# Second transposing split of a two-layer Flamingo block: context rows normalised by two engines, and earlier release of the latents' buffers

## What is computed

```python
x = x + tanh(g_xattn[0]) * L0_xattn_ref(_layernorm(x), ctx, ctx, W_q, W_k, W_v, W_o, b_o)
x = x + tanh(g_ffn[0])   * L0_ffn_ref(_layernorm(x), w1, conv_w, conv_b, w2)
x = x + tanh(g_xattn[1]) * L1_xattn_ref(ctx, _layernorm(x), mask, g_x, b_x, g_l, b_l, Wq, Wkv, Wout, g_o, b_o)
x = x + tanh(g_ffn[1])   * L1_ffn_ref(_layernorm(x), Wg, W1, W2, W3)   # top 2 of 8 experts

# inside L1_xattn_ref:
xn = layer_norm(ctx, g_x, b_x)           # context rows: mean, variance, gain, bias
ln = layer_norm(latents, g_l, b_l)       # latents: x after two layers
kv = concatenate([xn, ln], axis=1) @ Wkv
```

## Time and profile before

| | us |
|---|---|
| the three runs | 1301.79, 1304.35, 1304.62 |
| median | 1304.35 |
| the profiled execution, device time | 1301.08 |
| span of its trace | 1299.4 |
| second split in it, end of feed-forward to first matmul of the long stage | 424.9 to 463.2 |

### The profile page before, as it was taken

The page is one execution under the profiler, slowest core; times in us unless marked ns, Lnnn a source line. Parts: engine busy times, 40 slices in busy tenths (PEclk is TensorE's granted clock), DMA queues, the critical chain, the costliest instruction groups (busy, mean ns, idle before and its releaser), DMA issues.

```text
span 1299.4 us, 36455 instructions
## 1 busy us (share of the span) xinstructions
PE 1039.3 (80%) x13489; PEld 821.8 (63%) x13489; DVE 889.0 (68%) x2508; ACT 877.5 (68%) x1832; POOL 868.5 (67%) x983
## 2 busy tenths in 40 slices
PE   0569899994987379999999999999999982478760
PEld 0445677772544258888887878778787862356640
DVE  5689788885787767677676667667776763455545
ACT  0559899992665468888887878778888871355540
POOL 1170699993666747778678788788888886255561
PEclk9959655555999589999999999999999995698985
DMA  9995000000122001112212222121222211222216
GB/s 220 258 284 125 7 16 16 16 16 6 34 43 52 5 2 34 35 27 31 47 35 51 39 39 56 29 61 34 49 42 39 52 35 57 74 71 69 70 38 194
DMA packets 181539, 78.15 MB, mean 60 GB/s; under 512 B 116137, under 2 KB 177620, under 8 KB 181371
## 3 DMA queue, kind: packets, MB, share of 16 engines
q1 hardware_dynamic: 161563, 61.71, 21.9%
q0 software_dynamic: 4544, 8.67, 2.2%
q10 hardware_dynamic: 15264, 5.51, 1.7%
HBM read 19.54 MB, written 30.47 MB: 38 GB/s over the span
## 4 chain that ended last, share of the span: by engine, by line
PE 45%; POOL 5%; DVE 4%; issue 4%; another core or an unknown queue 3%; ACT 2%; DMA 1%; SPq 0%; POOLq 0%; ACTq 0%; DVEq 0%
PE bank L1428 12%; PE bank L1476 6%; PE bank L1462 4%; PE bank L1458 4%; PE bank L1459 4%; PE bank L1460 4%; PE bank L1502 3%; PE bank L2083 3%; PE bank L1447 3%; PE bank L2096 2%; POOL tokens L1321 1%; DVE X L2180 1%; POOL attention_pl_l L1221 1%; POOL attention_pl_c L1221 1%
## 5 line engine op out<-in xcount | busy, mean ns | idle before, releaser
L1748 DVE TENSOR_REDUCE attention_negmax<-bank 128x2 f16<-128x410 f32 x256 | 137.6, 579 | 141.6 <-PE bank L1447 141.6
L1221 POOL TENSOR_TENSOR attention_pl_l<-attention_probs_l,attention_ph_l 128x512 f16<-128x512 f32 x128 | 148.4, 1159 | 90.6 <-ACT attention_ph_l L1605 88.4
L637 POOL TENSOR_TENSOR attention_probs_l<-attention_probs,attention_probs_h 77x512 f16<-77x512 f32 x128 | 145.3, 1152 | 53.0 <-ACT attention_probs_h L719 48.8
L1221 POOL TENSOR_TENSOR attention_pl_c<-attention_probs_c,attention_ph_c 77x512 f16<-77x512 f32 x128 | 147.8, 1155 | 0.0
L2202 POOL DMA_INDIRECT outputs<-layer_kv x78 | 82.4, 1056 | 76.4 <-ACT layer_kv L2138 56.5
L1462 PEld LDWEIGHTS bank<-identh,attention_negmax 128*128 128x128 f16 (+1 forms) x1024 | 84.0, 108 | 56.6 <-issue 1.6
L1428 PE MATMUL bank<-layer_kv,ah 128*128 128x128 f16 x1024 | 108.2, 220 | 4.4 <-PEq L2315 4.2
L1476 PE MATMUL bank<-attention_vh_l,attention_ph_l 128*128 128x65 f16 x512 | 95.8, 195 | 18.0 <-POOL attention_pl_c L1221 18.0
L1428 PE MATMUL bank<-v1h,layer_kv 128*128 128x256 f16 (+1 forms) x512 | 106.3, 275 | 1.8 <-DVE attention_vl_c L1755 1.8
L1742 DVE SCALAR_TENSOR_TENSOR attention_tl<-bank,attention_th 128x512 f16<-128x512 f32 x128 | 87.7, 685 | 22.1 <-ACT attention_th L1596 21.9
L1605 ACT ACTIVATE attention_probs_l<-bank 128x512 f32<-128x512 f32 x128 | 76.2, 596 | 37.9 <-PE bank L1462 37.1
(11 more groups left out here) (378 smaller groups left out, 4132.6 us busy)
## 6 DMA issues: line engine op xcount, KB each, us to landing
tokens<-blank SPq DMA_DIRECT2D x1, 18360.0 KB, 70.9
layer_kv<-tokens SPq DMA_DIRECT2D x39, 136.0 KB
ctx<-outputs SPq DMA_DIRECT2D x8, 512.0 KB, 5.5
X<-in_x SPq DMA_DIRECT2D x4, 512.0 KB, 9.3
attention_pay<-attention_pay SPq DMA_DIRECT2D x8, 256.0 KB
out<-X ACTq DMA_DIRECT2D x8, 256.0 KB, 4.8
attention_turned_h<-attention_heads_h SPq DMA_TRANSPOSE x96, 2.2
attention_turned_l<-attention_heads_l SPq DMA_TRANSPOSE x96, 2.4
```

Of the source, the lines that this page charges most:

```text
L637: pool.tensor_tensor(probs_l[:, n % SLOTS], probs[:, n % 2], probs_h[:, n % SLOTS], ALU.subtract).then_inc(p_split, 1)
L1221: last = pool.tensor_tensor(low[:, g % 2], whole[:, g % 2], high[:, g % 2], ALU.subtract)
L1748: last = dve.tensor_reduce(negmax[:, g, 2 * i:2 * i + 2], score[i], AX.X, ALU.max, negate=True)
```

## The change

- The context's normalising goes from GpSimd alone to GpSimd and ScalarE: for each chunk GpSimd does batches 0 and 1 of the four (`first_half`, `tensor_scalar` as before) and ScalarE batches 2 and 3 (`second_half`, `activation` with Identity and the same scale and shift). TensorE waits for both (`ready` and a new semaphore `other`).
- ctx gets depth 4 in place of 2, with banks 0, 1, 6 and 7. The x job keeps banks 2 to 5.
- ScalarE does the second halves of chunks 0 and 1 ahead of its loop, and that of chunk k + 2 ahead of the copies of chunk k. GpSimd does the first halves of chunks 0 to 2 ahead of its loop, and that of chunk k + 3 ahead of the low part of chunk k.
- TensorE raises `turned` of all jobs at the start of its program, not when it comes to each job.

```diff
-            job.banks = [bank[2 * at + u][:, 0:CH * rows].rearrange("p (c r) -> p c r", r=rows) for u in range(job.depth)]
+            of = [0, 1, 6, 7] if job.by == "both" else [2 * at + u for u in range(job.depth)]
+            job.banks = [bank[i][:, 0:CH * rows].rearrange("p (c r) -> p c r", r=rows) for i in of]
...
         def _(pe):
             for job in jobs:
+                pe.sem_inc(job.turned, job.depth)
+            for job in jobs:
                 def turn(k, u):
-                    if job.by:
+                    if job.by == "both":
+                        pe.wait_ge(job.ready, k + 1)
+                        pe.wait_ge(job.other, k + 1)
+                    elif job.by:
                         pe.wait_ge(job.ready, k + 1)
...
-                pe.sem_inc(job.turned, job.depth)
                 chunks(pe, job, turn)
...
         def _(act):
+            def second_half(job, k):
+                u = k % job.depth
+                act.wait_ge(job.turned, k + 1)
+                for c in range(CH // 2, CH):
+                    one = slice(k * CH + c, k * CH + c + 1)
+                    last = act.activation(job.normed[:, u, c], job.src[:, k * CH + c], ACT.Identity, bias=job.shift[:, one],
+                                          scale=job.rstd[:, one])
+                last.then_inc(job.other, 1)
...
                     chunk = bass.ds(k * CH, CH)
+                    if job.by == "both" and k + 2 < NCH:
+                        second_half(job, k + 2)
                     act.wait_ge(job.turned, k + job.depth + 1)
...
+                if job.by == "both":
+                    second_half(job, 0)
+                    second_half(job, 1)
                 chunks(act, job, copy)
...
         def _(pool):
+            def first_half(job, k):
+                u = k % job.depth
+                pool.wait_ge(job.turned, k + 1)
+                for c in range(CH // 2):
+                    one = slice(k * CH + c, k * CH + c + 1)
+                    last = pool.tensor_scalar(job.normed[:, u, c:c + 1], job.src[:, one, :], job.rstd[:, one], job.shift[:, one],
+                                              ALU.mult, ALU.add)
+                last.then_inc(job.ready, 1)
...
                     chunk = bass.ds(k * CH, CH)
+                    if job.by == "both" and k + 3 < NCH:
+                        first_half(job, k + 3)
                     pool.wait_ge(job.high, k + job.depth + 1)
                     pool.tensor_tensor(job.lo(chunk), job.whole[:, u], job.hi(chunk), ALU.subtract).then_inc(job.split, 1)
-                    if job.by == "gpsimd" and k + 2 < NCH:
-                        normalise(pool, job, k + 2, u)
 
                 pool.sem_inc(job.split, job.depth)
-                if job.by == "gpsimd":
-                    normalise(pool, job, 0, 0)
-                    normalise(pool, job, 1, 1)
+                if job.by == "both":
+                    for k in range(3):
+                        first_half(job, k)
                 chunks(pool, job, low)
...
-                              "gpsimd", rstd=w.rstd_c, shift=w.shift_c, gain=gain_x, bias=bias_x),
+                              "both", rstd=w.rstd_c, shift=w.shift_c, gain=gain_x, bias=bias_x, depth=4),
```

More of the change, by code:

```diff
@@ L415, in split_transposed @@
             job.whole = m.sb(f"whole_{n}", [128, job.depth, CH, rows])
+            if job.by == "both":
+                job.other = m.sem(f"other_{n}")
             job.ready, job.turned, job.high, job.split = (m.sem(f"{x}_{n}") for x in ("ready", "turned", "high", "split"))
-            job.banks = [bank[2 * at + u][:, 0:CH * rows].rearrange("p (c r) -> p c r", r=rows) for u in range(job.depth)]
+            of = [0, 1, 6, 7] if job.by == "both" else [2 * at + u for u in range(job.depth)]
+            job.banks = [bank[i][:, 0:CH * rows].rearrange("p (c r) -> p c r", r=rows) for i in of]
         chain = m.sem("chain")
@@ L436, in normalise @@
                 one = slice(k * CH + c, k * CH + c + 1) if isinstance(k, int) else bass.ds(k * CH + c, 1)
-                if job.by == "gpsimd":
[L438 to L441, removed]
+                last = eng.tensor_scalar(job.normed[:, u, c:c + 1], job.src[:, one, :], job.mean[:, one, 0:1], job.rstd[:, one],
+                                         ALU.subtract, ALU.mult)
             last.then_inc(job.ready, 1)
```

## The result

The changed kernel took 1292.71 us (median of six runs, 1290.36 to 1294.54) against 1303.07 us for the kernel before (six runs, 1298.3 to 1304.62). The ratio is 0.9924, with an interval of 0.9908 to 0.994: faster by some 10 us, where 3.5 us were forecast and the range ended at 1296.5. The direction was right, the size wrong by a factor of three. (The kernel before was measured at 1304.35 us when the forecast was made and at 1303.07 us beside the changed kernel, so 1.3 us of the distance between 1300.9 and 1292.71 are the base.)

The account below looks back on a forecast made before the run. GpSimd on ctx, then VectorE on x, then the tail bound the second split. VectorE ending 3.2 us earlier and a tail 0.3 us shorter gave 3.5 us: 1304.35 - 3.5 = 1300.9 us, range 1296.5 to 1304.2.

Parts of the forecast that it names:

- What bounds the kernel: Between the feed-forward and the long stage, the path is GpSimd on ctx (2.48 us per chunk), VectorE on x, then the tail.
- tail: Second split, from VectorE's end on x to GpSimd's last low part: 3.9 us in place of 4.2, 0.3 us less.
- Release at once: Second split: VectorE begins x right behind its last small step, at 438.52 in place of 444.18, minus 5.66 us.
- ScalarE's share: Second split: ScalarE's added activations at 0.41 us each, two per ctx chunk, make its period 1.84 us, which sets ctx's pace.
- GpSimd's tensor_scalar do no such thing: Second split: GpSimd's tensor_scalar don't stall VectorE; L53 began inside four of them and took 0.22 us.
- The size of collisions: Each VectorE stall beside a GpSimd tensor_tensor costs 0.75 us on normalisings, by the first split, and 0.87 on small steps.
- small steps end: Second split: VectorE's small steps meet the low parts of ctx chunks 3 and 4, two collisions, and end at 438.5.
- 32 normalisings without collisions: Second split: VectorE's work on x with no stall, 32 x 0.29 = 9.28 us.
- collisions on x: Second split: VectorE's normalising of x meets three ctx and six x low parts, 9 at 0.75, 6.75 us.
- rival A: Collisions cost nothing extra: VectorE's stalls are bounded by the buffers or hide in its waits; gain 5.7 us, 1298.7, chance 0.15.
- The rest of the program shifts whole: The long stage is the same work with the same data, its first 3 us at the lower clock as now.
- rival D: Slower: a shifted start adds long-stage stalls with clock falls, 4.2 us each; one more 1305.1, two 1309.3; chance 0.07.

## Why the prediction was wrong

From the 1300.9 us that I gave to the measured 1292.71 it is 8.2 us: 1.3 are the base, 2.4 the second split, where the sum had too high a price for VectorE beside GpSimd, and some 4.5 the long stage, which the sum had as unchanged.

**What bounds the kernel: right.** The path through the second split was GpSimd on ctx, VectorE on x and the tail, and speeding up ctx shortened it.

**Release at once: right in sum, wrong in cause.** The 5.66 us of idle time went. I booked them on the release; without it they go as well, and alone it saves 2.05 us. The text itself had what was needed to see that: it had TensorE free for x before 438.5, which is when VectorE's small steps were to end. What the 5.87 us are made of is this: 5.66 of idle time gone, 0.9 of shorter small steps, less 0.66 for one more collision on x.

**ScalarE's share: right.** 0.43 us per instruction (0.41 taken), ctx chunks 1.76 us apart (1.84), last ctx low part from 439.63 (440.2), no wait on the new semaphore that cost anything.

**"GpSimd's tensor_scalar do no such thing": the step that failed in kind.** I read it off one instruction, L53, that ran free, as did the five behind it. But the two slow steps of the same rows speak against it: L1103 and L57 began at 433.81 and 436.29, the `tensor_tensor` only at 434.11 and 436.59. At 0.2 us each they would have been done before it began, had the last `tensor_scalar` ahead of it not held them. With four buffers on GpSimd alone a hold went on through four `tensor_scalar`. When they hold VectorE and when they don't stays open.

**The size of collisions: the step that failed in the sum.** Its terms against the trace:

| term | predicted | measured |
|---|---|---|
| small steps end | 438.5 | 437.6 (held by 0.44 twice, not 0.87) |
| 32 normalisings without collisions | 32 x 0.29 = 9.28 | 8.2 (0.257 each) |
| collisions on x | 9 x 0.75 = 6.75 | 3 x 0.49 + 5 x 0.91 = 6.0 |
| VectorE on x in all | 16.0 | 14.24 |
| tail | 3.9 | 4.2 |

The measured collisions are the long instructions of the trace less the 0.333 of a free one (0.82 or 0.83 beside ctx, 1.23 to 1.26 beside x); the pace is what is left, (14.24 - 6.0) / 32. The pace of 0.29 and the price of 0.75 came from the first split: the pace is too slow and the price of a collision beside x too low, and the two errors cancelled for the 13.58 us of the kernel before, which the sum therefore seemed to explain. It counted six collisions there; the trace has seven, and eight in the changed kernel, not nine. The three differences are 0.9 + 1.8 - 0.3 = 2.4 us, and 3.5 + 2.4 is the 5.9 of the trace. The nearest of my cases for the split was rival A, 5.7 us, and not by luck alone: what x lost by one more collision (0.66 us) was less than what the small steps gained (0.9).

**The rest of the program shifts whole: wrong by more than that.** Two executions differ by up to three falls of the clock in attention, 597 to 600 us for the same kernel. I had the rows for it in rival D, but used them only for a slower kernel, and put the stall itself into the price; the stalls are there in every trace, and the fall alone costs 1.0 to 2.1 us. The range should have carried that scatter on the fast side: the lower end would have been 1298.7 - 4 = 1294.7 and still short of the 1292.7 that came. (By the terms it names, the range began at 1298.7 - 2.6 = 1296.1 rather than 1296.5, which changes nothing here.) Even with the right split, 1303.07 - 5.9 = 1297.2 would have been 4.5 us too high, and of these only a part is traced to falls.

## What to carry to other kernels

Before you book a wait on the semaphore that ended it, ask when the engine behind it would have been ready anyway: here the release looked like the cure, and with half of GpSimd's normalising on ScalarE it wasn't needed. When VectorE has a chain of short dependent instructions, take GpSimd's work away from beside it rather than queue more: prefetching deeper on GpSimd made this stage slower than before. A price and a pace fitted to one mix of work can be wrong in both; check them against the durations of single instructions. Before a gain of some microseconds is read out of two traces, look whether the clock fell equally often in both.

## What the runs showed of the hardware

- VectorE held by GpSimd: an instruction of 0.19 us took 3.06 us beside a `tensor_tensor`, four `tensor_scalar` and another `tensor_tensor` of GpSimd. In the kernel before, six small steps in a row ran free (0.18 to 0.22 us each) beside four `tensor_scalar`.
- The Trainium skill, SBUF — State Buffer, section "Who interferes with whom", describes the shared ports as an exclusive lock that one of the two engines has for a whole instruction. The rows agree for single holds: with four buffers on GpSimd alone, three small steps took 0.67 us each beside `tensor_tensor`s of 0.75. They also have a hold that lasted over several instructions and small steps that weren't held at all.
- One more collision of a 128x128 normalising costs VectorE 0.49 us beside the `tensor_tensor` of ctx and 0.91 us beside that of x.
- GpSimd is slowed as well: four `tensor_scalar` in 1.98 us beside VectorE's normalising, 1.78 beside the small steps.
- After a stall of TensorE of 2.1 to 2.5 us its clock fell to 1.2 GHz for 3.4 us in some executions and in others not, for the same kernel and the same stall. With one such fall the work up to the next stall took 1.0 to 1.3 us longer on two chips and 1.8 to 2.1 us on others.
- The same kernel took 1256.8 us on one chip and 1298.5 on another. The difference lies behind attention, where rows are gathered and scattered by DMA: from the end of attention to the end of the span it is 194.2 us in a trace of before on the one and 234.3 on the other, and between 1100 and 1200 us the DMA moved 84 and then 101 GB/s on the one and 73 and then 70 on the other (means of 50 us). That the DMA is the cause isn't shown. Up to the end of attention the two agree within 2 us.
